# A two-layer transformer kernel: four linear recurrences in one stage, with the norms of the next sequence laid between their units, then four feed-forwards in one stage

## The reference, cut to what matters

```python
def L0_attn(x, ...):                       # its x is already layernorm(x) of the caller
    y = layernorm(x, ln1_g, ln1_b)
    q, k, v = y @ Wq + bq, y @ Wk + bk, y @ Wv + bv        # 1024 channels each
    g = sigmoid(y @ Wg + bg)
    state_t = decay * state_{t-1} + k_t * v_t              # over the 1024 tokens
    out_t   = g_t * q_t * state_t * 64 ** -0.5
    x2 = x + out @ Wo + bo
    h = layernorm(x2, ln2_g, ln2_b)
    return x2 + gelu(h @ W1 + b1) @ W2 + b2                # 512 hidden
```

## Time and profile before

| what | us |
|---|---|
| median of 3 timed runs | 2621.07 (2618.85 to 2622.15) |
| the profiled execution's own time | 2596.13 |
| its span, first to last instruction | 2594.0 |
| first `recurrence` begins to the mixture's first norm | 27.5 to 390.2 |
| mean granted TensorE clock | 0.877 of full speed |

### The profile page before, as it was taken

One profiled execution on the slowest core, in us unless ns is written; L12 is line 12 of the kernel. 1 busy time (PEld: TensorE's weight loads), 2 busy tenths in 40 slices (PEclk: granted clock), 3 DMA queues, 4 the chain that ended last, 5 costly groups with the idle time before them and its releaser, 6 DMA issues. The chain is left out here.

```text
span 2594.0 us, 46050 instructions
## 1 busy us (share of the span) xinstructions
PE 2041.2 (79%) x16904; PEld 963.5 (37%) x16904; DVE 2003.5 (77%) x3416; ACT 1503.4 (58%) x2914; POOL 567.4 (22%) x692
## 2 busy tenths in 40 slices
PE   6889883694449999999999669999999998359910
PEld 5678663673212222222222322222222222259910
DVE  6676765766678999999996689999999993576635
ACT  3434431142125998989889317998989897105510
POOL 2232220275630000000000250000000000006555
PEclk9999995697677999999999769999999999559955
DMA  4000001035360101111000250110110100302211
GB/s 187 1 0 0 0 0 40 27 98 95 92 184 16 32 24 37 31 30 32 23 23 11 92 165 19 30 41 20 32 42 19 41 6 15 110 7 72 66 50 55
DMA packets 94392, 120.92 MB, mean 47 GB/s; under 512 B 23664, under 2 KB 56560, under 8 KB 93936
## 3 DMA queue, kind: packets, MB, share of 16 engines
q1 hardware_dynamic: 73712, 78.92, 10.9%
q0 software_dynamic: 8960, 18.37, 3.0%
q10 hardware_dynamic: 11520, 20.98, 2.6%
HBM read 69.70 MB, written 42.99 MB: 43 GB/s over the span
## 5 line engine op out<-in xcount | busy, mean ns | idle before, releaser
L1274 DVE TENSOR_REDUCE mx<-psum 128x1 f32<-128x1024 f32 x1024 | 1174.6, 1215 | 79.0 <-PE psum L1162 78.1
L1251 ACT ACTIVATE p<-psum 128x512 f32<-128x512 f32 x2048 | 1102.3, 596 | 107.5 <-PE psum L1184 65.0
L1196 PE MATMUL psum<-p,v_ext 128*32 128x256 f32 x8192 | 655.6, 392 | 39.3 <-ACT p L1251 39.3
L1162 PE MATMUL psum<-ks,qs 64*128 64x512 bf16 x2048 | 635.2, 394 | 52.5 <-DVE mx L1274 30.1
L1184 PE MATMUL psum<-qs,ks 64*128 64x512 bf16 x2048 | 629.8, 383 | 1.4 <-ACT p L1251 1.2
L1196 PEld LDWEIGHTS psum<-p,v_ext 128*32 128x32 f32 x8192 | 161.9, 108 | 473.7 <-ACT p L1251 254.9
L1184 PEld LDWEIGHTS psum<-qs,ks 64*128 64x128 bf16 x2048 | 123.5, 93 | 403.3 <-ACT p L1251 367.3
L1064 POOL CAST m_near<-mx 128x16 bf16<-128x16 f32 x128 | 25.1, 196 | 1080.5 <-DVE mx L1274 1076.3
L605 ACT ACTIVATE hid<-psum,stage 128x128 f32<-128x128 f32 x448 | 132.1, 366 | 180.6 <-PE psum L575 180.6
L549 POOL DMA_INDIRECT x_in<-n_rows,token_of x152 | 166.8, 1098 | 250.3 <-POOLq L85 183.2
L1162 PEld LDWEIGHTS psum<-ks,qs 64*128 64x128 bf16 x2048 | 118.7, 94 | 114.5 <-DVE mx L1274 81.3
(11 more groups left out here) (192 smaller groups left out, 2108.4 us busy)
## 6 DMA issues: line engine op xcount, KB each, us to landing
qs<-qk_parts SPq DMA_DIRECT2D x128, 104.0 KB
ks<-qk_parts SPq DMA_DIRECT2D x128, 104.0 KB
qk_parts<-piece__1 ACTq DMA_DIRECT2D x40, 256.0 KB, 3.7
qk_parts<-piece__2 ACTq DMA_DIRECT2D x40, 256.0 KB, 3.3
answers<-y_out SPq DMA_DIRECT2D x152, 64.0 KB, 1.6
ew<-in_moe SPq DMA_DIRECT2D x1, 5136.0 KB, 19.2
ew<-in_moe SPq DMA_DIRECT2D x1, 4624.0 KB, 14.7
n_rows<-xn SPq DMA_DIRECT2D x8, 512.0 KB, 3.2
```

The source lines that it names most:

```text
L1162: pe.matmul(psum[:, bank, :], a["qs"][r, g % NKF, j % KM, i * P:(i + 1) * P], a["ks"][r, g % NKF, j % KM, k * HALF:(k + 1) * HALF], start= ...
L1196: last = pe.matmul(psum[GR * j:GR * j + VW, O_BANK, q], t["v_ext"][:, b * NT + i, VE * (h0 + j):VE * (h0 + j) + VW], a["p"][:, (GH * s + j ...
L1251: act.activation(a["p"][:, n % NP, :], psum[:, S_BANK + n % NS, :], ACT.Exp, scale=DH ** -0.5)\
L1274: dve.tensor_reduce(a["mx"][:, g % 2, h, j, 0, c:c + 1], psum[:, bank:bank + 2, :].rearrange("p a c -> p (a c)"), AX.X, ALU.max)\
```

## The change

The loop over sequences is gone. `recurrence` runs the 64 units of all four sequences without a break. The norm of sequence b + 1 is cut into steps, which VectorE runs behind given units of sequence b: statistics behind unit 1, aggregation behind 2, the reciprocal chain behind 4, four scalings each behind 5, 6, 7 and 8, the low halves of the split inputs behind 11 and 13. ScalarE takes the square root behind unit 3 and the copies behind 9 and 11; TensorE transposes behind 8 and 10; GpSimd adds the output bias behind unit 10. The sum of a finished sequence (`sum_up`) is done behind unit 2 of the next. One PSUM bank now belongs to the transposes, so the projections go round five instead of six; `LAG` is 3 and `gated` has 4 buffers; y_high and y_low are doubled. x2 of every sequence is kept (in `n_all`, which is free at that time).

Then one stage `feed_forward` does all four sequences. Its norm of x2 (ln2) is no longer in the recurrence stage but here, one sequence ahead. GpSimd's eight adds stand in a row at its start, without a wait for anyone else.

```diff
 def recurrence(nc, t, w, x, x2):
-    units = [(c, h) for c in range(CH) for h in range(NH)]
-    NB, LAG, BANKS = 3, 2, 6
+    units = [(b, c, h) for b in range(B) for c in range(CH) for h in range(NH)]
+    NB, LAG, BANKS, T_BANK, OUT = 4, 3, 5, 5, 6
...
         def _(pe):
             for u in range(len(units) + LAG):
                 if u < len(units):
                     project(u)
+                    b, at = divmod(u, UB)
+                    if b + 1 < B and at in (8, 10):
+                        turn(b + 1, (at - 8) // 2)
                 if u >= LAG:
                     output(u - LAG)
-            norm_tensor(pe, t, sems, t["xn"])
...
         def _(act):
...
-            norm_scalar_root(act, t, sems)
-            norm_scalar_copy(act, t, sems, t["y_t"], col("ln2_g"), col("ln2_b"))
+                if b + 1 < B:
+                    if u % UB == 3:
+                        root(b + 1)
+                    if u % UB in (9, 11):
+                        copy_turned(b + 1, (u % UB - 9) // 2)
...
         def _(dve):
+            def prepare(b, at):
+                if at == 1:
+                    for i in range(NT):
+                        last = dve.bn_stats(t["stats"][:, i, :], x[b][:, i, :])
+                    link(last)
...
+                elif at in (5, 6):
+                    for i in range(TPH * (at - 5), TPH * (at - 4)):
+                        dve.tensor_scalar(t["yn"][:, i, :], x[b][:, i, :], t["mv"][:, i, 0:1], t["rstd"][:, 1, i:i + 1],
+                                          ALU.subtract, ALU.mult).then_inc(tile_ready, 1)
...
+                if b and u % UB == 2:
+                    sum_up(b - 1)
+                if b + 1 < B:
+                    prepare(b + 1, u % UB)
+            sum_up(B - 1)
...
-def feed_forward(nc, t, w):
+def feed_forward(nc, t, w, x, x2):
...
+            turn(0)
+            for b in range(B):
+                up(b)
+                if b + 1 < B:
+                    turn(b + 1)
+                down(b)
...
         def _(act):
+            root(0)
+            copy_turned(0)
+            for b in range(B):
+                if b + 1 < B:
+                    root(b + 1)
+                for n in range(NF):
+                    f, h = n // NH, n % NH
+                    act.wait_ge(hidden, NF * b + n + 1)
+                    if b and f == 0:
+                        act.wait_ge(out_done, NT * (b - 1) + TPH * (h + 1))
+                    act.activation(t["ffh"][:, f, h * HALF:(h + 1) * HALF], psum[:, n % 4, :], ACT.Gelu,
+                                   bias=col("b1", f)).then_inc(gelued, 1)
+                if b + 1 < B:
+                    copy_turned(b + 1)
...
         def _(pool):
-            link(pool.tensor_tensor(t["x"](), t["x"](), t["x2"][:, :, :], ALU.add))
-            link(pool.tensor_tensor(t["x"](), t["x"](), t["row"]("b2"), ALU.add))
+            for b in range(B):
+                pool.tensor_tensor(x[b], x[b], t["row"]("b2"), ALU.add).then_inc(b2_added, 1)
+                pool.wait_ge(b2_added, b + 1)
+                pool.tensor_tensor(x[b], x[b], x2[b], ALU.add).then_inc(x_added, 1)
...
         def _(dve):
+            norm(0)
+            for b in range(B):
+                if b + 1 < B:
+                    norm(b + 1)
+                dve.wait_ge(x_added, b + 1)
+                for h in range(NH):
+                    dve.wait_ge(out_done, NT * b + TPH * (h + 1))
+                    s = slice(h * TPH, (h + 1) * TPH)
+                    dve.tensor_tensor(x[b][:, s, :], psum[:, OUT + h, :].rearrange("p (a d) -> p a d", d=D),
+                                      x[b][:, s, :], ALU.add).then_inc(x_summed, 1)
...
-            with nc.Fori(0, B) as b:
-                t["x"], t["x_next"] = view(x_all, b), view(x_all, (b + 1) % B)
-                recurrence(nc, t, w)
-                feed_forward(nc, t, w)
+            x, x2 = ([tiles[:, b * NT:(b + 1) * NT, :] for b in range(B)] for tiles in (x_all, n_all))
+            recurrence(nc, t, w, x, x2)
+            feed_forward(nc, t, w, x, x2)
```

More of the change, by code:

```diff
@@ L249, in project @@
             def project(u):
-                c, h = units[u]
+                b, c, h = units[u]
+                if b and c == 0:
+                    pe.wait_ge(low, NH * (b - 1) + h + 1)
                 for i, m in enumerate((2, 1, 3, 0)):
@@ L270, in output, with turn @@
                 last.then_inc(out_done, 1)
+            def turn(b, half):
+                if NH * (b - 1) + half:
+                    pe.wait_ge(y_copied, NH * (b - 1) + half)
+                pe.wait_ge(tile_ready, NT * (b - 1) + TPH * (half + 1))
+                for i in range(TPH):
+                    last = pe.transpose(psum[:, T_BANK, i * P:(i + 1) * P], t["yn"][:, half * TPH + i, :], t["ident"][:, :])
+                last.then_inc(turned, 1)
             for u in range(len(units) + LAG):
@@ L343, in _, with turn @@
         @block.tensor
         def _(pe):
[L345 to L358, removed]
+            def turn(b):
+                for i in range(NT):
+                    if b and i % TPH == 0:
+                        pe.wait_ge(y_copied, NH * (b - 1) + i // TPH + 1)
+                    pe.wait_ge(tile_ready, NT * b + i + 1)
+                    pe.transpose(psum[:, T_BANK + i // TPH, (i % TPH) * P:(i % TPH + 1) * P], t["xn"][:, i, :],
+                                 t["ident"][:, :]).then_inc(turned, 1)
@@ new lines, in up, with down @@
+            def up(b):
+                for n in range(NF):
+                    f, h = n // NH, n % NH
+                    if NF * b + n >= 4:
+                        pe.wait_ge(gelued, NF * b + n - 3)
+                    pe.wait_ge(y_copied, NH * b + h + 1)
+                    pe.matmul(psum[:, n % 4, :], w.w1[:, f * P:(f + 1) * P], t["y_ff"][b % 2][:, h * HALF:(h + 1) * HALF],
+                              start=True, stop=True).then_inc(hidden, 1)
+            def down(b):
+                pe.wait_ge(gelued, NF * (b + 1))
+                for i in range(NT):
+                    if b and i % TPH == 0:
+                        pe.wait_ge(x_summed, NH * (b - 1) + i // TPH + 1)
+                    for f in range(FF):
+                        last = pe.matmul(psum[:, OUT + i // TPH, (i % TPH) * P:(i % TPH + 1) * P],
+                                         t["ffh"][:, f, i * P:(i + 1) * P], w.w2[:, f, :],
+                                         start=(f == 0), stop=(f == FF - 1))
+                    last.then_inc(out_done, 1)
@@ L377, in _ @@
         @block.vector
         def _(dve):
[L379 to L386, removed]
+            link = chain(dve, step)
@@ L1383, in build @@
             t["yn"], t["y_f"] = sb("yn", [P, NT, D], where=scope), sb("y_f", [P, L], where=scope)
[L1384 removed]
+            t["y_high"], t["y_low"] = ([sb(n, [P, L], F32R, where=scope) for _ in range(2)] for n in ("y_high", "y_low"))
+            t["y_ff"] = t["y_t"], t["y_f"]
             loads = [(t["ffh"][:, i, :], w0_in[i]) for i in range(4)]
```

121 lines of the change are left out of this document (89 added, 32 removed).

## The result

| kernel | median of the timed runs, us | runs |
|---|---|---|
| before, same chip | 2621.61 (2618.85 to 2624.83) | 4 |
| after | 2599.61 (2594.71 to 2602.38) | 4 |

A forecast was written before the change was run, and what follows sets the result against it. TensorE sets the pace in the units; 118.1 us behind them can gain. Recurrence 253.0, barrier 1.1 and feed-forward 92.5 make 346.6 against 362.7, so 2580.0 profiled; with 25 us carried over 2605.0, range 2592 to 2614.

The forecast's parts named there:

- TensorE's own work in the recurrence: Recurrence stage: TensorE's units, slow start, transposes for three next sequences and the end together take 240.5 us.
- VectorE's units in a preparing sequence: Recurrence, first three sequences: units 1 to 8 take VectorE 33.5 to 36.5 us against TensorE's 29.5.
- the ends 4.2 and 4.95: Units 5 to 8: 4.2 us if GpSimd waits out four scalings, 4.95 if it enters behind the first; taken 4.6.
- TensorE's stalls: Recurrence: TensorE waits for a late VectorE, 8 to 17 us over three sequences, taken 12.5.
- norm(0) behind the adds: Feed-forward start: GpSimd's eight adds hold VectorE's norm(0), which ends after 19.7 to 22.0 us, taken 21; alone 6.0.
- N to the end of down(0): Feed-forward, from norm(0)'s end (N) through the first down matmuls: 18.8 us, first four up matmuls at a low clock.
- Middle periods: Feed-forward, two periods from down to down: sum, statistics, root and table, Gelu, down; 17.7 us each, 35.4 together.
- no change that can be told: Rival: upper-end stalls and norm(0), plus a TensorE clock fall in each middle period; gain 5.6 us, 2615.5; chance 0.08.
- The table load before the Gelus: ScalarE, feed-forward: load of 1.28 us without the skill's extra drain; with a drain the time would be 2609.1.
- adds that hold nothing: Rival, feed-forward start: GpSimd's eight adds do not hold norm(0), N is 6.4 us; time 2590.4; chance 0.10.
- a VectorE that never holds TensorE: Rival, recurrence: the norm's steps fill VectorE's idle time, no 12.5 us of stalls; time 2592.5; chance 0.10.
- the slower rival: Rival: TensorE stays at 1.2 GHz through the feed-forward stage, +45 us, time 2650; chance 0.04.

The follow-up runs named there:

- act_scale: Changed kernel with the 16 scalings of units 5 to 8 moved from VectorE to ScalarE; 2561.89 us, ratio to the kernel before 0.9871.
- adds_late: Changed kernel with GpSimd's two adds per sequence waiting until the norms in front of them are through; 2560.04 us, ratio to the kernel before 0.9862.
- after_again: Changed kernel without edit, timed again beside the kernel before; 2571.43 us, ratio 0.9907.
- after_third: Changed kernel without edit, timed with the second group beside the kernel before; 2572.15 us, ratio 0.9912.
- adds_quarter: Changed kernel with each of GpSimd's eight adds split into four of 128x256; 2566.35 us, ratio to the kernel before 0.9888.
- root_early: Changed kernel with the feed-forward's later norms and their roots placed earlier, ahead of sums and Gelus; 2568.16 us, ratio to the kernel before 0.9896.

## Why the prediction was right

The time, 2599.6, lies inside the range, near its middle, 5.4 us under the 2605.0. The block shows the same: 341.6 against the forecast 346.6. One part of the 2605.0 no row had given: I carried over the 25 us between the profile of the kernel before and its timed runs. In this timing they did appear, in the changed kernel's own profile too (2256.0 us behind the block for 2231.3). In the two later timings neither kernel has them: there 2605.0 would have been 33 us too high, with a gain as large as here. That the time came out is in part luck; the test of the reasoning is the block. By the steps:

- **TensorE's own work in the recurrence, 240.5.** Right within a microsecond: act_scale, where TensorE hardly waits, has 239.6.
- **VectorE's units in a preparing sequence.** From multiply to multiply, second sequence: behind unit 1 4.24 us (I had 4.3), behind 2 with the sum 4.65 (5.0), behind 3 3.13 (3.14), behind 4 4.82 (4.85), behind 5 to 8 4.57 to 4.64 (4.6). The next eight take 27.3 us (28.0): the splits cost less than 0.69 each, since the scan behind them meets less of GpSimd (3.60 and 3.47 for 3.8). Between the ends 4.2 and 4.95 the mechanism was that of the upper one: GpSimd's multiply starts at 51.72, behind the first scaling, and the other three wait. The Trainium skill has it so (SBUF — State Buffer, Who interferes with whom: the first holds the ports for one whole instruction), and here the trace agrees. The size was below the upper end: the hold is 2.10 - 1.07 = 1.03 us, not 1.25, and the rest of the unit is 4.58 - 2.10 = 2.48, not 2.62. That the middle of the two ends fits was luck, no reason led to it.
- **TensorE's stalls, 12.5 (8 to 17).** 250.1 - 240.5 = 9.6 by my own terms, 10.5 by act_scale. TensorE waits for kv 14 times in the first three sequences and never in the fourth, as forecast. This is the first mis-sized term, 2 to 3 us too high: a middle sequence of VectorE is 62.5 us where my terms gave 63.6.
- **norm(0) behind the adds, 21 (19.7 to 22.0).** 20.0, and adds_late shows the 14 us that they cost. The count was not as I had it. I let five small steps hold an add each, and the scalings one or two. Three small steps were held (280.42, 282.18, 284.68). Two ran at 0.17 in the gap between two adds (279.74, 284.47; the adds start at 279.78 and 284.49). The eight scalings waited for four adds. Either way VectorE gets out only when the eight adds are nearly through, so the sum was right for a different split.
- **N to the end of down(0), 18.8.** Measured 17.3, from 297.37 to 307.25 + 7.41. The first eight matmul records up took 4.75 us, not 6.31 as in the earlier trace rows: the granted clock was back at 1.00 some 2 us behind their start, where it had taken some 5. In the kernel before TensorE stood idle for 1.51 us ahead of them; here they follow the transposes at once. That the transposes come spread out here (at 289.28, 291.69, 293.99 and five from 296.41) is not the reason: in adds_late all eight come in one group, and the 16 up matmuls take the same 8.72 us. Whether the missing gap is the reason no run shows. This is the second mis-sized term, 1.5 us.
- **Middle periods, 35.4.** 36.4: 17.34 for one, as predicted (17.7), and 19.05 for the other, in which the granted clock was low. The window over it in the changed kernel:

```profile
320.00:326.00 6.00, 5.88 (x14) 2.81 (x15) 1.29 (x6) 4.31 (x8) 0.00 (x0) 0.72 0.00 0
```

That is part of the rival "no change that can be told": I had put 2.5 us on a fall in each middle period. It came in one of two, at 5.40 - 3.70 = 1.7 us, and in the same one (5.38 to 5.40) in after_again, after_third, adds_late, adds_quarter and act_scale. root_early, without the 2.02 us wait, has neither the wait nor the fall.
- **The table load before the Gelus.** 318.08 to 319.36, the Gelu at 319.38, as in the earlier trace rows. ScalarE in the changed kernel:

```profile
318.08 1.28 ACT L487 ACT_TABLE_LOAD   x1
319.38 2.42 ACT L487 ACTIVATE ffh<-psum,cols 128x512 f32<-128x512 f32 x4
```

The drain that the Trainium skill adds to a switch (ScalarE: Activation LUTs, What ACT_TABLE_LOAD costs) is not in these rows; the measurement decides, at 1.28 us for the load.
- **The rest.** Last period 15.06 (15.4), from there to the mixture's norm 1.7 (1.95).

In sum the terms of the block were 5.0 us too high: 2.9 in the recurrence stage (253.0 for 250.1; by act_scale 0.9 of it is TensorE's own work and 2.0 the stalls), 1.0 in norm(0), 1.5 behind it, -1.0 in the middle periods, 0.3 in the last, 0.3 behind it. Beyond the block 1 to 4 us of the timed gain have no place in the traces. As for the rivals: adds that hold nothing (2590.4) and a VectorE that never holds TensorE (2592.5) are refuted by adds_late and act_scale, and TensorE stayed at full clock for most of the stage (0.87 of full speed in the mean), so the slower rival did not come.

## What to carry to other kernels

Merging stages takes away the waits at their ends, but what stood alone there now meets the neighbour on the shared ports. Count, for each small linked step, up to one whole instruction of the other engine, and ask whether that engine's work is due at all then; here one wait that puts eight adds later gave 11 us, and cutting them in four gave 6. Give small elementwise work to an engine that has room and isn't held (here ScalarE, busy 27.4 of 62.5 us in a sequence, with 0.41 us a scaling beside the multiply), and put a late root behind work that is ready, not ahead of it.

## What the runs showed that I had not expected

- A held VectorE instruction waits for one GpSimd instruction, be it long or short: 2.26 us for a step of 0.17 beside adds of 2.34, 1.24 beside a multiply of 1.27, 0.65 beside adds of 0.69. But not each is held: of five small steps, two ran at 0.17 in the gap between two adds.
- The same 80 expert tiles took 127.9 us in one execution and 108.6 to 109.6 in nine others, with the same matmuls, and the kernel before took 2621 us in one timing and 2595 to 2597 in two others. Only times taken side by side can be compared.
- TensorE's granted clock fell in the first middle period of the feed-forward and not in the second, though both have the same wait of 2.02 us, and this was so in all six profiles with that wait. Why only there stays open.
